# Three node tiles turned by transposing DMAs in place of TensorE, in a one-core graph-network kernel

## The reference

```
agg = segment_sum(x[src], dst)                       # sum over neighbours
h   = (1 + eps) * x + agg                            # "h0"
h   = relu(batch_norm(h @ W1 + b1))                  # 512 -> 1024
h   = relu(batch_norm(h @ W2 + b2))                  # 1024 -> 512
x   = layernorm(x + (x + h))
h   = relu(x @ lW1 + lb1) @ lW2 + lb2                # 512 -> 256 -> 512
x   = layernorm(x + h + segment_sum(h[src], dst))
```

## Time and profile before

| what | value |
|---|---|
| median of 3 runs | 254.96 us (254.82 to 254.99) |
| the profiled execution | 255.28 us |
| its span, first to last instruction | 253.1 us |
| mean granted TensorE clock | 0.970 of 2.4 GHz |
| TensorE busy | 231.9 us (92%) |
| VectorE busy | 159.3 us (63%) |
| ScalarE busy | 134.0 us (53%) |
| GpSimd busy | 84.5 us (33%) |

### The profile page before, as it was taken

How to read it: one execution, slowest core, us unless ns; L and a number is a source line. 1 busy time by engine, 2 the same in 40 slices (tenths; PEclk the granted TensorE clock), 3 DMA queues, 4 the chain that set the end, 5 groups by cost and what they waited for, 6 DMA issues and landing times.

```text
span 253.1 us, 3841 instructions
## 1 busy us (share of the span) xinstructions
PE 231.9 (92%) x1433; PEld 199.4 (79%) x1433; DVE 159.3 (63%) x369; ACT 134.0 (53%) x226; POOL 84.5 (33%) x75
## 2 busy tenths in 40 slices
PE   0837999999999999999999999999999699999991
PEld 0826998777888888888888888888889698888970
DVE  1769799873966343455555237361789989685374
ACT  0726674654867067454555406353735537935473
POOL 5510000003920006565655400404096449501241
PEclk9975999999999999999999999999999889999998
DMA  4378600000066501111000195505049900000334
GB/s 107 143 228 223 165 3 0 4 0 5 0 261 245 181 0 44 41 41 41 3 0 0 29 213 104 104 3 104 1 78 162 209 0 0 3 0 0 128 123 157
DMA packets 32323, 19.96 MB, mean 79 GB/s; under 512 B 21928, under 2 KB 27085, under 8 KB 32303
## 3 DMA queue, kind: packets, MB, share of 16 engines
q1 hardware_dynamic: 31796, 19.45, 29.2%
q0 software_dynamic: 160, 0.13, 0.2%
q10 hardware_dynamic: 346, 0.10, 0.2%
HBM read 8.51 MB, written 5.92 MB: 57 GB/s over the span
## 4 chain that ended last, share of the span: by engine, by line
PE 66%; DVE 14%; DMA 7%; ACT 7%; issue 2%; SPq 1%; POOL 1%; DVEq 0%
PE ps L1249 22%; PE ps L1193 17%; PE ps L1312 9%; PE ps L1330 6%; PE ps L1266 5%; PE ps L1279 4%; DMA plane_T<-planes 3%; DVE xT L964 2%; DVE hot_s L817 2%; PE ps L1173 2%; ACT xr L678 2%; DMA src_i<-in_src 2%; DMA pairs<-pair 2%; ACT planes L669 1%; DVE small_t L919 1%
## 5 line engine op out<-in xcount | busy, mean ns | idle before, releaser
L919 DVE BATCH_NORM_STATS2 small_t<-ps 128x6 f32<-128x500 f32 (+1 forms) x36 | 21.6, 600 | 41.4 <-PE ps L1249 25.2
L1193 PE MATMUL ps<-AT,xh 128*128 128x500 f32 (+2 forms) x120 | 43.2, 370 | 0.0
L1193 PE MATMUL ps<-AT,xl 128*128 128x500 f32 (+2 forms) x120 | 41.4, 355 | 0.0
L1249 PE MATMUL ps<-h0h,wh 128*128 128x500 f32 (+1 forms) x96 | 33.9, 353 | 0.0
L1249 PE MATMUL ps<-h0h,wl 128*128 128x500 f32 (+1 forms) x96 | 33.9, 353 | 0.0
L1249 PE MATMUL ps<-h0l,wh 128*128 128x500 f32 (+1 forms) x96 | 33.8, 352 | 0.0
L470 POOL TENSOR_TENSOR wl<-w1s,wh 128x512 fp32r<-128x512 f32 x8 | 10.1, 1302 | 47.2 <-ACT AT L544 47.2
L475 POOL TENSOR_TENSOR wl<-w2s,wh 128x512 fp32r<-128x512 f32 x8 | 11.1, 1384 | 43.9 <-ACT wh L646 43.9
L1193 PEld LDWEIGHTS ps<-AT,xh 128*128 128x128 f32 (+1 forms) x120 | 23.1, 192 | 2.7
L1193 PEld LDWEIGHTS ps<-AT,xl 128*128 128x128 f32 (+1 forms) x120 | 23.1, 192 | 2.7
L544 ACT ACTIVATE AT<-ps 128x500 fp32r<-128x500 f32 x25 | 14.7, 590 | 18.4 <-PE ps L1173 18.1
(11 more groups left out here) (144 smaller groups left out, 497.7 us busy)
## 6 DMA issues: line engine op xcount, KB each, us to landing
turns<-half_out SPq DMA_DIRECT2D x10, 320.0 KB, 2.2
out<-x SPq DMA_DIRECT2D x9, 256.0 KB
w1s<-in_L_gnn_W SPq DMA_DIRECT2D x4, 512.0 KB, 6.0
w2s<-in_L_gnn_W SPq DMA_DIRECT2D x8, 256.0 KB, 2.8
xs<-in_x SPq DMA_DIRECT2D x1, 1280.0 KB, 7.8
xs<-in_x SPq DMA_DIRECT2D x1, 1024.0 KB
lws<-in_L_gnn_W SPq DMA_DIRECT2D x1, 512.0 KB, 4.9
lw2s<-in_L_gnn_W SPq DMA_DIRECT2D x1, 512.0 KB, 4.2
```

The lines of the kernel that those rows point to most:

```text
L919: link(nc.vector.bn_stats(stats[:, 6 * c:6 * c + 6], ps[:, zbank(t, c), 0:c1 - c0]))
L1193: last = mm(o, part[0:r, k, d * P:d * P + P], AT[0:r, k, c0:c1], start=(k == 0 and j == 0), stop=(k == NT - 1 and j == 1))
L1249: last = mm(ps[:, zbank(t, c), 0:c1 - c0], w[:, t, d * P:d * P + P], h[c][:, d, :], start=(d == 0 and j == 0), stop=(d == DT - 1 and j == 2))
```

## The change

Tiles 7, 8 and 9 are no longer turned by x_cols and x_turn; tiles 0 to 6 (XD = 7) still are. In groups 6 and 7 ScalarE copies the low and the high halves of tiles 7 and 8 to two 16-bit planes (x_to_plane), in groups 11 and 12 those of tile 9. When all four copies are done, SP issues two transposing DMAs from SBUF to SBUF, one for each plane (twelve 128x128 blocks each). In groups 19 to 22 ScalarE writes the four results into the halves of xT (x_late), behind a wait for both DMAs. The planes lie where h0 of the last 500 nodes will be written later. GpSimd clears the last tile's rows of both planes at the start. The waits that named all ten tiles now name seven, h0_own of unit 8 waits for the late copies, and the first w1_high waits for the plane copies, since W1's tiles lie over x.

```diff
+        XD = NT // 2 + 2
+        R_XD = R_H0 + 24 * KB
+        x_plane = [at(f"x_plane{i}", [P, NT - XD, D], I16, R_XD + i * (NT - XD) * D * 2) for i in range(2)]
+        x_plane_T = [at(f"x_plane_T{i}", [P, (NT - XD) * DT, P], I16, R_XD + (2 + i) * (NT - XD) * D * 2) for i in range(2)]
...
-        cols_at = {6: half + 2, 7: half + 3, 11: half + 4}
-        turn_at = {6: half + 2, 7: half + 3, 12: half + 4}
+        plane_at = {6: (XD, NT - 1, 0), 7: (XD, NT - 1, 1), 11: (NT - 1, NT, 0), 12: (NT - 1, NT, 1)}
+        late_at = {19: (XD, NT - 1, 0), 20: (XD, NT - 1, 1), 21: (NT - 1, NT, 0), 22: (NT - 1, NT, 1)}
...
@@ sync, behind the loads of w1
+            sp.wait_ge(x_plane_set, len(plane_at))
+            for i in range(2):
+                sp.dma_start_transpose(x_plane_T[i][:, :, :], x_plane[i][:, :, :].rearrange("p t d -> p (t d)")
+                                       ).then_inc(x_planes_T, 16)
...
@@ gpsimd, behind the memsets of half_out
+            for t in x_plane:
+                nc.gpsimd.memset(t[:, NT - 1 - XD, :], 0).then_inc(x_pad, 1)
...
@@ scalar
+            def x_to_plane(k0, k1, i):
+                r = rows[k1 - 1]
+                act.wait_ge(x_in2, 32)
+                act.wait_ge(x_pad, 2)
+                nc.scalar.activation(x_plane[i][0:r, k0 - XD:k1 - XD, :], half_of(xs[0:r, k0:k1, :].rearrange(
+                    "p t d -> p (t d)"), i).rearrange("p (t d) -> p t d", d=D), ACT.Copy).then_inc(x_plane_set, 1)
+
+            def x_late(k0, k1, i):
+                c0, c1 = P * k0, min(P * k1, N)
+                act.wait_ge(x_planes_T, 32)
+                src = x_plane_T[i][:, (k0 - XD) * DT:(k1 - XD) * DT, 0:min(P, c1 - c0)].rearrange(
+                    "p (t d) c -> p d t c", d=DT)
+                out = xT[:, :, c0:c1].bitcast(I16).rearrange("p d (t c i) -> p d t c i", i=2, t=k1 - k0)[:, :, :, :, i]
+                nc.scalar.activation(out, src, ACT.Copy).then_inc(xT_late, 1)
...
-                    act.wait_ge(x_turned, NT)
+                    act.wait_ge(x_turned, XD)
+                    act.wait_ge(x_plane_set, len(plane_at))
...
-                    if g in turn_at:
-                        x_turn(turn_at[g])
+                    if g in plane_at:
+                        x_to_plane(*plane_at[g])
+                    if g in late_at:
+                        x_late(*late_at[g])
...
@@ vector, h0_own
-                    v.wait_ge(xT_set, NT)
+                    v.wait_ge(xT_set, XD)
+                if i == NI - DT:
+                    v.wait_ge(xT_late, len(late_at))
...
@@ tensor
-                        pe.wait_ge(xT_set, NT)
+                        pe.wait_ge(xT_set, XD)
...
-                    if g in cols_at:
-                        x_cols(cols_at[g])
```

More of the change, by code:

```diff
@@ L179, in gnn_kernel @@
         par_r = tmp("par_r", [P, P], F32)
+        XD = NT // 2 + 2
+        R_XD = R_H0 + 24 * KB
+        x_plane = [at(f"x_plane{i}", [P, NT - XD, D], I16, R_XD + i * (NT - XD) * D * 2) for i in range(2)]
+        x_plane_T = [at(f"x_plane_T{i}", [P, (NT - XD) * DT, P], I16, R_XD + (2 + i) * (NT - XD) * D * 2) for i in range(2)]
+        assert TMP[0] <= R_XD and R_XD + 4 * (NT - XD) * D * 2 <= R_W and R_XD >= R_H0 + 2 * DT * CH[2][0] * 4
         ident = misc("ident", [P, P], F32)
@@ L227, in gnn_kernel @@
         x_turned, xT_set, h0_own_set = sem("x_turned"), sem("xT_set"), sem("h0_own_set")
+        x_pad, x_plane_set, x_planes_T, xT_late = (sem(n) for n in ("x_pad", "x_plane_set", "x_planes_T", "xT_late"))
         stored = sem("stored")
@@ L344, in gnn_kernel @@
         w1_at = {CHG[1] + t: t for t in range(HT)}
-        assert EARLY == half and NT == half + 5 and max(cols_at) < CHG[1] and CHG[1] + HT <= NG and 2 + DT <= x_bank(half)
+        assert EARLY == half and NT == half + 5 and max(plane_at) < CHG[1] <= min(late_at)
+        assert CHG[1] + HT <= NG and 2 + DT <= x_bank(half) and CH[1][1] <= XD * P
         def h0_after(g):
@@ L595, in _ @@
             with act.Else():
-                for k in turn_at.values():
-                    x_turn(k)
+                for part in plane_at.values():
+                    x_to_plane(*part)
+                for part in late_at.values():
+                    x_late(*part)
                 for k in high_at.values():
@@ L1210, in _ @@
                         aggregate(*u)
-                    if g in cols_at:
-                        x_cols(cols_at[g])
             with pe.Else():
-                for k in cols_at.values():
-                    x_cols(k)
-                pe.wait_ge(xT_set, NT)
+                pe.wait_ge(xT_set, XD)
                 pe.wait_ge(gen_zero, 1)
```

## The result

The changed kernel takes 256.34 us (median of 5 runs, 256.01 to 256.99) against 254.86 of the kernel before (median of 5, 254.27 to 254.99). The ratio is 1.0061, with a 95% interval of 1.0039 to 1.0084: 1.5 us slower, where 0.8 us less was forecast. The profiled span is 254.2 us against 253.1. Times within the span are those of one profiled execution of each kernel.

What follows compares the result with a forecast made beforehand. TensorE was taken to bound from 38.87 to 149.03 us, with ScalarE and VectorE before; xh(6) 0.81 us earlier passes through VectorE to build(14), other costs covered: 254.96 - 0.8 = 254.2 us, range 253.8 (and 0.05 for measurement) to 254.95.

Steps and rivals of the forecast that it cites:

- The three x_cols and the merge with VectorE: Groups 7 to 14: TensorE issues 1.22 us less, waits 1.0 before builds 12 to 14; 0.81 reaches build(14).
- TensorE's 1.22 us: Time TensorE no longer spends on the transposes of tiles 7, 8 and 9; no gain by itself.
- The plane copies: ScalarE, groups 6 and 7: 1.03 us per full copy, yet xh(6) at 30.58, 0.81 us earlier.
- The transposing DMAs: Issued on SP at about 36.2, landed at 42.2, asked for at about 49.0 us; fully covered.
- rival 4: Planes land late, ahead of build(22): 262 us at four times the row, about 269 by the skill page; chance 0.03.
- ScalarE in groups 19 to 22: Late copies of 1.32 us, slots of 1.3, AT(20) at 50.8, AT(21) at 53.6; no cost on the path.
- 0.8 us less at build(14), nothing given back: The sum: the 0.8 us gained at build(14) carries over to the end, giving 254.2 us.
- whatever moves 38.87 moves everything behind it: From build(14) at 38.87 us on, later stages are gated by TensorE, so a shift there carries through.
- The chain of waits: Profile's waits from the touched groups to the end; TensorE alone named from 38.87 to 149.03 us.
- Rival 5: Something else absorbs or adds within noise of placement, split between same and slower; chance 0.06.

Runs made afterwards that it cites:

- b_pad232: The kernel before with 116 small products (232 instructions) added at the start, where TensorE idles: 258.10 us, ratio 1.0128.
- a_elsepad48: The changed kernel with 24 small products (48 instructions) written into TensorE's never-run Else body: 255.30 us, ratio to before 1.0020.
- a_pad12: The changed kernel with 6 small products (12 instructions) at TensorE's start: 253.38 us, ratio to before 0.9958.
- a_pad24: The changed kernel with 12 small products (24 instructions) ahead of TensorE's first wait: 254.18 us, ratio to before 0.9979.
- b_elsepad80: The kernel before with 40 small products (80 instructions) in TensorE's never-run Else body: 254.87 us, ratio 1.0017.
- b_noelse: The kernel before without TensorE's Else body: 253.46 us, ratio 0.9940.
- a_pad48: The changed kernel with 24 small products (48 instructions) at TensorE's start: 253.19 us, ratio to before 0.9935.
- a_layout24: The changed kernel with 48 instructions of small products at TensorE's start and 24 in its never-run Else body: 255.02 us, ratio to before 1.0006.
- a_layout: The changed kernel with 12 small products at TensorE's start and 12 in its never-run Else body: 253.60 us, ratio to before 0.9955.

## Why the prediction was wrong

Right, by its own steps:

- **The three x_cols and the merge with VectorE.** From build(6), build(8) came 2.58 us later (2.56 forecast) and build(14) 11.28 (12.08 before). In front of builds 12, 13 and 14 TensorE waited 0.2, 0.4 and 0.4 us, as said. TensorE's 1.22 us became 0.80 at build(14), since VectorE's alternation of x_low and one_hots ended last, with hot_k as releaser.
- **The plane copies.** 1.05 us each (1.03), xh(6) at 30.39, which with the 0.19 is the 30.58 of the text.
- **The transposing DMAs.** Issued at 36.2 as worked out, landed about 41.5 (42.2 forecast), 7 us before they were asked for. The Trainium skill (VectorE: DVE Perf Modes, The three transpose paths) gives 1309 ns for one block by DMA, and rival 4 took from it an estimate of 31 us for 24 blocks. The trace doesn't bear this out as a price for each block: it had about 5.3 us for all of them.
- **ScalarE in groups 19 to 22.** 1.37 us for a late copy (1.32), slots of 1.23 (1.3), AT(20) at 50.57 and AT(21) at 53.24, 0.2 and 0.4 ahead of the text, of which 0.2 is the execution's own. TensorE didn't wait.

Wrong is the step "0.8 us less at build(14), nothing given back", and with it the sentence in the first part that whatever moves 38.87 moves everything behind it. The chain of waits names TensorE alone up to 149.03, but that chain holds for the code as it was laid out. TensorE's next instruction must also have been fetched, which the chain of an execution where it was in time doesn't show. The removed transposes were costed by their 1.22 us of busy time alone; that they are also 24 instructions, in front of a jump over some 350 (160 products of two instructions each, and two loops), wasn't costed. (The `Else` body has lost its own copy of them, another 24, so the code behind the jump lies 48 instructions further ahead.) In the kernel before, the code behind the jump was ready at about 61.75, by the estimate above, for a product at 61.95. In the changed kernel the fetch began 0.5 us later by the span's time, took 0.35 longer, and TensorE came to the jump 1.0 earlier: some 1.9 in all, of which the margin covers 0.2; 1.68 were lost. Rival 5 named placement, but as noise of 0.2%, with 0.03 for slower; it had neither the place nor the size.

That the idle is at the jump and hangs on where the code lies is shown four ways: it goes with 12, 24 or 48 instructions more in front of the jump, it goes without the body that is jumped over, it stays when the body grows, and it comes up in the kernel before, once by 232 instructions in front and once by 80 that are never run. That the thing waited for is a fetch is read from the packets, whose ends lie 1.5 to 1.7 us ahead of the product in all four kernels; no run delayed a packet by itself. The profile's releaser, VectorE's h0l, was an inference from what had just ended: in b_pad232 the same idle has "issue".

The second loss, a fetch within a pair of transposes, is shown by 5 pairs against 23 and by one edit that foretold it (a_elsepad48, 6.08 to 4.99). The third, VectorE's update behind GpSimd's cast, is shown by 3 kernels against 11, with no run that moved the cast alone. Neither was in the forecast: behind 149.03 the chain of before goes through VectorE, ScalarE and the pairs of transposes, and there the step "whatever moves 38.87 moves everything behind it" took their times as fixed.

The Trainium skill states the first of the losses (Runtime: NRT & Kernel Launch, Instruction fetch mechanics): a taken branch whose target isn't in the pages held must wait for a DMA of that page. The traces agree, with 1.28 to 1.68 us lost. It could have been a rival: the trace of before shows a fetch that ends 1.8 us ahead of the product at 61.95. That 1.6 us of these are needed is shown by the trace after alone.

The profiled spans understate the loss (1.1 against 1.5 timed). In the profiled execution of before the granted clock was at 1.2 GHz from 200.6 to 204.0, on the chain, and TensorE did 24 products from 200 to 204 against 36 in the 4 us behind; after, it was so from 193.4 to 196.8, where TensorE worked too, but the chain went through VectorE until 203.6. So part of the 1.97 us that the stage gives back is this fall's.

What stays open. What begins a fetch: a_pad12 shows that it doesn't move in step with the instructions. What the fetch at 191 to 195 costs: the stage takes 17.34 to 17.54 us in the 7 kernels without one and 17.82 to 21.56 in the 7 with one, but there the clock's fall is mixed in for three (before, a_pad24 and a_pad12), and the 21.56 of a_pad12 are of the execution that took 3.0 us more than the median. It is likely the second loss again: in each of the 7 with one, one of the two half_out transposes took 2.11 to 3.21 us in SP's rows, in the 7 without, 1.39 to 1.76. It fits the time of b_elsepad80, which has the idle at the jump and is as fast as before, and the gain of b_noelse, but no run moved this fetch alone. And a_pad48 is 1.5 us faster than before, with a change worth 0.8; where the rest comes from isn't shown.

## What to carry to other kernels

An edit that adds or removes instructions on an engine also moves its code, and in front of a far jump that is a term of the sum: look in the trace of before for how long ahead of the jump the last instruction fetch ended. A few small products where the engine idles, or in the body that isn't run, test it in one run; here the change with 48 instructions of padding takes 253.19 us, 1.5 less than before, while the change as it was made takes 256.34. Nothing here shows that the same padding helps another kernel: a_layout24, with 24 instructions more than a_layout, lost what a_layout had won. Compare two versions only where the fetches fall alike, or count each one's misfortunes first, and don't take a releaser at a jump for a cause. And where two engines start at nearly the same time, as VectorE and GpSimd at 184 us, a delay of 1 us ahead of one of them can cost a second.

## What the runs showed of the hardware

- In four kernels with idle at the far jump, TensorE's next product started 1.5 to 1.7 us after the end of a 16 KB instruction packet, which itself took 0.9 to 1.3 us; 1.28 to 1.68 us were lost.
- One such packet that began within a pair of transposing DMAs (5.0 us) made the pair 0.6 to 1.2 us longer, in 5 of 5 cases.
- VectorE's update of 1250 columns took 1.46 us where it began before a cast of GpSimd, and 2.37 to 2.49 where the cast had begun 0.05 to 0.17 us earlier.
- Padding of 0, 12, 24 and 48 instructions gave 256.34, 253.38, 254.18 and 253.19 us: the first 12 brought about 3 us, more than the change itself. The intervals of the runs with 12 and 24 overlap.
- Two transposing DMAs of 12 blocks each from SBUF to SBUF took about 5.3 us from issue to landing.
